# Two of the 64 score strips of a head get their exponentials on VectorE, with a new order of the strips, of the quantisation and of the FFN weight's decoding

## What is computed

```python
x = x + attn(layernorm(x))            # 8 key/value heads, each with 4 query groups, head size 16
x = x + ffn(layernorm(x))

# attn
q, k, v = x @ Wq.T, x @ Wk.T, x @ Wv.T
scores = einsum('bsqhd,bthd->bqhst', qh, kh) * 0.25
a_dot = softmax(scores) @ vh
a_mem = elu(q) @ memory / (elu(q) @ memory_norm)
out = a_dot * (1 - w) + a_mem * w     # w = sigmoid(memory_weight)

# ffn: one 512x512 product
x_fp8 = clip(x / s).astype(float8_e4m3fn)
y = (x_fp8 * s) @ (weight_fp8 * weight_scale).T
```

## Time and profile before

| what | value |
|---|---|
| three runs | 2145.21, 2145.61, 2146.34 us; median 2145.61 |
| the profiled execution's own time | 2146.34 us |
| its span, first to last instruction | 2144.2 us |
| mean granted TensorE clock | 0.994 |
| ScalarE busy | 1991.7 us (93%) |
| PE matmul records busy | 2086.2 us (97%) |
| VectorE busy | 483.7 us (23%) |
| GpSimd busy | 71.2 us (3%) |
| exponentials (L590) | 2112 instructions, 1882.6 us busy |
| scores (L692) | 16384 matmuls, 1149.5 us busy |
| weighing by v (L703) | 8192 matmuls, 1058.4 us busy |

### The profile page before, as it was taken

How to read it: one execution, slowest core, us unless ns; L and a number is a source line. 1 busy time by engine, 2 the same in 40 slices (tenths; PEclk the granted TensorE clock), 3 DMA queues, 4 the chain that set the end, 5 groups by cost and what they waited for, 6 DMA issues and landing times.

```text
span 2144.2 us, 65931 instructions
## 1 busy us (share of the span) xinstructions
PE 2086.2 (97%) x27314; PEld 779.5 (36%) x27314; DVE 483.7 (23%) x1006; ACT 1991.7 (93%) x2308; POOL 71.2 (3%) x93
## 2 busy tenths in 40 slices
PE   7999799999999999999999999999999999999996
PEld 4555333333333333333333333333333333333332
DVE  5666410013011311131110311130112211131104
ACT  4544699999999999999999999999999999999995
POOL 3222000000000000000000000000000000000000
PEclk9999899999999999999999999999999999999998
DMA  5554311111111211121111211111112111121111
GB/s 185 174 178 139 108 46 46 44 45 31 40 44 44 64 34 30 44 64 44 44 32 37 64 44 44 41 46 41 44 44 64 39 30 44 44 64 44 27 37 40
DMA packets 119531, 124.69 MB, mean 58 GB/s; under 512 B 13696, under 2 KB 96000, under 8 KB 119488
## 3 DMA queue, kind: packets, MB, share of 16 engines
q1 hardware_dynamic: 117424, 121.42, 20.6%
q10 hardware_dynamic: 2064, 2.69, 0.4%
HBM read 86.57 MB, written 37.49 MB: 58 GB/s over the span
## 4 chain that ended last, share of the span: by engine, by line
PE 68%; ACT 14%; issue 13%; DVE 3%; SPq 1%; DMA 0%; POOL 0%; DVEq 0%; ACTq 0%
PE ps L692 32%; PE ps L703 28%; ACT pool L590 13%; PE ps L640 4%; PE ps L735 1%; PE ps L654 1%; DVE pool L833 1%; PE ps L616 1%; DVE parts L858 0%; DVE norm L862 0%; DVE y_out L920 0%; SPq L299 0%; SPq L311 0%; DMA y_out<-in_Wq 0%; DVE ps L925 0%
## 5 line engine op out<-in xcount | busy, mean ns | idle before, releaser
L590 ACT ACTIVATE pool<-ps 128x1024 f32<-128x1024 f32 (+1 forms) x2112 | 1882.6, 1172 | 13.9 <-PE ps L692 13.6
L692 PE MATMUL ps<-q_st,k_st 99*32 99x512 bf16 x16384 | 1149.5, 380 | 13.7 <-DMA v_st<-v_aug 10.1
L703 PE MATMUL ps<-pool,v_st 128*32 128x512 f32 x8192 | 1058.4, 592 | 0.7 <-ACT pool L590 0.7
L692 PEld LDWEIGHTS ps<-q_st,k_st 99*32 99x32 bf16 x16384 | 375.1, 95 | 988.2 <-ACT pool L590 673.8
L703 PEld LDWEIGHTS ps<-pool,v_st 128*32 128x32 f32 x8192 | 247.2, 111 | 205.3 <-ACT pool L590 1.6
L1006 DVE STREAM_TRANSPOSE by_token<-ps 128x512 f32<-128x512 f32 x64 | 45.9, 717 | 421.6 <-PE ps L703 421.6
L1092 DVE RECIPROCAL rnorm<-ps 128x2 f32<-128x2 f32 x64 | 10.9, 170 | 519.1 <-PE ps L735 519.1
L1060 DVE SCALAR_TENSOR_TENSOR y_out<-ps,scalars,resid 128x512 f32 x28 | 21.0, 751 | 449.8 <-PE ps L721 449.8
L640 PE MATMUL ps<-pool,wqT 128*128 128x512 f32 x256 | 113.9, 592 | 0.0
L546 ACT ACTIVATE parts<-ps 128x512 bf16<-128x512 f32 x40 | 23.9, 597 | 75.6 <-PE ps L640 75.6
L640 PEld LDWEIGHTS ps<-pool,wqT 128*128 128x128 f32 x256 | 47.9, 190 | 52.5 <-issue 50.2
(11 more groups left out here) (114 smaller groups left out, 599.3 us busy)
## 6 DMA issues: line engine op xcount, KB each, us to landing
q_st<-q_aug SPq DMA_DIRECT2D x384, 64.0 KB
v_st<-v_aug SPq DMA_DIRECT2D x64, 256.0 KB
...
```

Of the source, the lines that this page charges most:

```text
L590: act.activation(probs[:, j % PTILES, q * CH:(q + len(strips)) * CH], sc[v % SLOTS][:, 0:len(strips), :].rearrange("p a b -> p (a b)"), AC ...
L692: last = pe.matmul(sc[u % SLOTS][VW * c:VW * c + VW, x, :], k_st[0:AUG, par, keys:keys + VW], q_st[0:AUG, par, q * CH:q * CH + CH], start= ...
L703: last = pe.matmul(acc[par][VW * c:VW * c + VW, :].rearrange("v (i s) -> v i s", s=VW), v_st[:, par, j, :], by_place[:, c, :, :], start=(j ...
```

## The change

Units. The table of a head's units is now a list of 33 triples (tile, first strip, number of strips). Tiles 0, 1 and 2 come first (units 0 to 5), then tile 15 ("late") as unit 6 with two strips and units 7 and 8 with one strip each, then tiles 3 to 14 (units 9 to 32). ScalarE takes the 31 units with two strips. Units 7 and 8 are VectorE's: `late_exps` reads each strip from PSUM (with a maximum against a lower limit), which frees its slot, and then computes the exponentials of both strips at once, 128x1024, with two instructions of one input and six of two inputs. `slot_free` says whom PE waits for before it overwrites a slot. ScalarE's scale is changed and W_k is scaled to fit, so that VectorE can build a power of two from the score directly.

Order. The weighing of tile 15 is moved to unit 26, between those of tiles 9 (at 25) and 10 (at 27); the other places are in `WEIGH_AT`. The ring has 3 tiles and one place of its own for tile 15. The memory products go to units 11 and 24, the FFN's transposition to unit 6 and its products to units 9, 11, 12 and 14.

Quantisation. VectorE rounds a tile of 128 tokens in each pair of heads, between the two halves of the memory term; GpSimd works out one tile's standard deviation at a time. The weight is decoded by a quarter (128x512) in each of the chunks 1 to 4 of the preparation, and is transposed by PE and copied by ScalarE after the last chunk. The polynomial's scratch lies over `parts`, so VectorE waits for the stores of `parts` before the heads.

The diff, cut to its core:

```diff
+LATE = 2
 SLOTS = 3
-UNIT_STRIPS = [(i, i + 1) for i in range(0, STRIPS - UNIT, UNIT)] + [(STRIPS - 2,), (STRIPS - 1,)]
+LATE_TILE = ST - 1
+BEFORE_LATE = 3
+RING = 3
+
+
+def units_of_head():
+    def halves(j):
+        return [(j, 0, 2), (j, 2, 2)]
+
+    units = [u for j in range(BEFORE_LATE) for u in halves(j)]
+    units += [(LATE_TILE, 0, 2), (LATE_TILE, 2, 1), (LATE_TILE, 3, 1)]
+    return units + [u for j in range(BEFORE_LATE, LATE_TILE) for u in halves(j)]
+
+
+UNIT_STRIPS = units_of_head()
 UNITS = len(UNIT_STRIPS)
-PTILES = 4
...
+BY_ACT = [u for u, (_, _, n) in enumerate(UNIT_STRIPS) if n == 2]
+BY_DVE = [u for u, (_, _, n) in enumerate(UNIT_STRIPS) if n == 1]
+HEAD_EXPS = len(BY_ACT)
+LAST_UNIT = {j: u for u, (j, _, _) in enumerate(UNIT_STRIPS)}
+
+WEIGH_AT = {4: 0, 6: 1, 10: 2, 26: LATE_TILE} | {LAST_UNIT[j] + SLOTS: j for j in range(BEFORE_LATE, LATE_TILE)}
...
+DECODE_STEPS = 8
+FLOAT8_STEPS = 6
+FFN_TURN_AT = 6
+FFN_PRODUCT_AT = (9, 11, 12, 14)
+MEMORY_AT = (11, 24)
...
-        probs = pool[:, 0:PTILES * QG * CH].rearrange("p (a b) -> p a b", a=PTILES)
+        probs = pool[:, 0:RING * QG * CH].rearrange("p (a b) -> p a b", a=RING)
+        late_probs = pool[:, RING * QG * CH:(RING + 1) * QG * CH]
...
+        late = parts[:, :, :, :].rearrange("p o i s -> p (o i s)").bitcast(F32)
+        late_x, late_z, late_p = (late[:, i * LATE * CH:(i + 1) * LATE * CH] for i in range(3))
...
-                act.activation(dst, src, ACT.Copy).then_inc(w_copied, 1)
+                act.activation(dst, src, ACT.Copy, scale=SCALE / EXP_UNIT if j == KT else 1.0).then_inc(w_copied, 1)
...
+                else:
+                    for k in range(KT):
+                        act.wait_ge(wf_turned, k + 1)
+                        act.activation(wT_ffn[:, k, :], weight_tp[k % 2], ACT.Copy).then_inc(wf_copied, 1)
...
-                    strips = UNIT_STRIPS[v % UNITS]
-                    j, q = divmod(strips[0], QG)
-
-
-                    act.wait_ge(scores_ready, pair * (2 * UNITS) + v + 1)
-                    act.activation(probs[:, j % PTILES, q * CH:(q + len(strips)) * CH],
-                                   sc[v % SLOTS][:, 0:len(strips), :].rearrange("p a b -> p (a b)"), ACT.Exp,
-                                   scale=SCALE).then_inc(probs_ready, 1)
+                for par in range(2):
+                    for a, u in enumerate(BY_ACT):
+                        j, q, n = UNIT_STRIPS[u]
+                        held = late_probs if j == LATE_TILE else probs[:, j % RING, :]
+
+
+                        act.wait_ge(scores_ready, pair * (2 * HEAD_EXPS) + par * HEAD_EXPS + a + 1)
+                        act.activation(held[:, q * CH:(q + n) * CH], sc[u % SLOTS].rearrange("p a b -> p (a b)"), ACT.Exp,
+                                       scale=EXP_UNIT).then_inc(probs_ready, 1)
...
+                    turn_ffn_weight()
+
+            def turn_ffn_weight():
+                pe.wait_ge(dec, KT * DECODE_STEPS)
+                for k in range(KT):
+                    if k >= 2:
+                        pe.wait_ge(wf_copied, k - 1)
+                    for a in range(KT):
+                        last = pe.transpose(weight_tp[k % 2][:, a * P:a * P + P], w_val[:, a, k * P:k * P + P], ident_bf[:, :])
+                    last.then_inc(wf_turned, 1)
...
+            def slot_free(n, u):
+                v = (u - SLOTS) % UNITS
+                heads_back = 1 if u < SLOTS else 0
+                if v in BY_DVE:
+                    pe.wait_ge(late_taken, n * LATE + BY_DVE.index(v) + 1)
+                else:
+                    pe.wait_ge(probs_ready, n * HEAD_EXPS + BY_ACT.index(v) + 1 - heads_back * HEAD_EXPS + THREE_FREE)
+
...
-                pe.wait_ge(probs_ready, n * UNITS + u - SLOTS + 1 + THREE_FREE)
-                for x, strip in enumerate(UNIT_STRIPS[u]):
...
+                last.then_inc(late_scores if u in BY_DVE else scores_ready, 1)
...
+                if j == LATE_TILE:
+                    pe.wait_ge(late_ready, n + 1)
+                held = late_probs if j == LATE_TILE else probs[:, j % RING, :]
...
+                        if u in WEIGH_AT:
+                            weigh_v(n, par, WEIGH_AT[u])
+                        elif u + UNITS in WEIGH_AT and not (first and par == 0):
+                            weigh_v(n - 1, 1 - par, WEIGH_AT[u + UNITS])
...
+            def decode_weight(a):
+                first = a * DECODE_STEPS
+                mag, sign, twice = (work[:, 4 + i, :] for i in range(3))
+                if a == 0:
+                    dve.wait_ge(w8_loaded, 16)
...
+                dve.tensor_tensor(w_val[:, a, :], mag, sign, ALU.mult).then_inc(dec, 1)
...
+                    if o == 3 and 1 <= c < 1 + KT:
+                        decode_weight(c - 1)
...
+            for o in range(QG + 1):
+                dve.wait_ge(parts_stored[o], 16 * SPLIT * (NG + 1))
+
+            def late_exps(n):
+                for d, u in enumerate(BY_DVE):
+                    dve.wait_ge(late_scores, n * LATE + d + 1)
+                    dve.tensor_scalar(late_x[:, d * CH:d * CH + CH], sc[u % SLOTS][:, 0, :], LOWEST, None, ALU.max)\
+                        .then_inc(late_taken, 1)
+                dve.wait_ge(late_taken, n * LATE + LATE)
+                dve.tensor_scalar(late_z, late_x, ROUND, None, ALU.add).then_inc(late_step, 1)
+
+                dve.wait_ge(late_step, n * LATE_STEPS + 1)
+                dve.scalar_tensor_tensor(late_x, late_z, ROUND, late_x, ALU.subtract, ALU.subtract).then_inc(late_step, 1)
+
+
+                dve.wait_ge(late_step, n * LATE_STEPS + 2)
+                dve.tensor_scalar(late_z.bitcast(I32), late_z.bitcast(I32), 23, LEADING_BITS,
+                                  ALU.logical_shift_left, ALU.bitwise_or).then_inc(late_step, 1)
+                dve.scalar_tensor_tensor(late_p, late_x, POWER[4], late_x, ALU.add, ALU.mult).then_inc(late_step, 1)
+                for i in (3, 2, 1):
+                    dve.wait_ge(late_step, n * LATE_STEPS + 7 - i)
+                    dve.scalar_tensor_tensor(late_p, late_p, POWER[i], late_x, ALU.add, ALU.mult).then_inc(late_step, 1)
+                dve.wait_ge(late_step, n * LATE_STEPS + LATE_STEPS)
+                dve.scalar_tensor_tensor(late_probs[:, LATE * CH:2 * LATE * CH], late_p, POWER[0], late_z, ALU.add, ALU.mult)\
+                    .then_inc(late_ready, 1)
...
+                dve.tensor_tensor(xq_now[:, :], xs, big, ALU.subtract).then_inc(xq_ready, 1)
...
+            with dve.Fori(0, HEADS // 2) as hp:
+                late_exps(2 * hp)
+                add_memory(0, hp, 0)
+                add_memory(0, hp, 1)
+                add_head(2 * hp, 0, 0, 2 * hp)
+                late_exps(2 * hp + 1)
+                add_head(2 * hp + 1, 1, 0, 2 * hp + 1)
...
             with dve.Fori(1, NG) as g:
-                round_to_float8(g - 1)
                 with dve.Fori(0, HEADS // 2) as hp:
-                    add_memory(g, hp)
-                    next_ffn_tile(g - 1, hp)
+                    late_exps(g * HEADS + 2 * hp)
+                    add_memory(g, hp, 0)
+                    round_to_float8(g - 1, hp)
+                    add_memory(g, hp, 1)
                     add_head(g * HEADS + 2 * hp, 0, g, 2 * hp)
+                    take_turned(g - 1, hp)
+                    late_exps(g * HEADS + 2 * hp + 1)
                     ffn_out(g - 1, hp)
                     add_head(g * HEADS + 2 * hp + 1, 1, g, 2 * hp + 1)
             chunk_moments(NG - 1)

```

More of the change, by code:

```diff
@@ L1 @@
+import math
 from contextlib import ExitStack
@@ L158, in attention_ffn @@
         tp = [ps[:, i, :] for i in (0, 1)]
+        weight_tp = [ps[:, i, 0:CH // 2].bitcast(BF16) for i in (0, 1)]
         pj = [ps[:, i, :] for i in (2, 3, 5, 6)]
@@ L162, in attention_ffn @@
         k_norm = (vp[:, 0:1], n2[:, 0:1])
-        sc = [ps[:, UNIT * i:UNIT * i + UNIT, :] for i in range(SLOTS)]
+        sc = [ps[:, 2 * i:2 * i + 2, :] for i in range(SLOTS)]
         acc = [ps[:, i, :] for i in (6, 7)]
@@ L684, in _ @@
                 pe.wait_ge(gm_loaded, 16 * QK_LOADS * (NG * HEADS + 1) + 32)
+            def slot_free(n, u):
[3 more added lines that the diff above has]
+                    pe.wait_ge(late_taken, n * LATE + BY_DVE.index(v) + 1)
+                else:
+                    pe.wait_ge(probs_ready, n * HEAD_EXPS + BY_ACT.index(v) + 1 - heads_back * HEAD_EXPS + THREE_FREE)
             def scores(n, par, u):
-                pe.wait_ge(probs_ready, n * UNITS + u - SLOTS + 1 + THREE_FREE)
-                for x, strip in enumerate(UNIT_STRIPS[u]):
-                    j, q = divmod(strip, QG)
+                slot_free(n, u)
+                j, q0, count = UNIT_STRIPS[u]
+                for x in range(count):
+                    q = q0 + x
                     for c in range(P // VW):
@@ L737, in memory_products, with pair @@
                 last.then_inc(am_ready, 1)
-            def turn_ffn_weight(k):
-                if k == 0:
```

(31 more changed lines are left out.)

164 lines of the change are left out of this document (72 added, 92 removed).

## The result

The changed kernel takes **2178.96 us** (median of 4 runs, 2176.77 to 2179.47), the kernel before 2145.58 in the runs beside it: a ratio of 1.0153, 95% interval 1.0136 to 1.0171. It is slower by 33 us, where 19 were forecast. The profiled execution took 2179.47 us with a span of 2177.8; before, these were 2146.34 and 2144.2. So some 33.5 us of the span are to be explained.

The account below looks back on a forecast made before the run. ScalarE was taken as the bound, PE close behind. Heads +11.1, preparation +8 and smaller terms +0.2 on the profiled 2146.34 us gave 2165.6, median put at 2165 us, range 2150 to 2182.

Parts of the forecast that it names:

- The restart behind unit 6: Each head: ScalarE has nothing after unit 6 until unit 9 is written; 0.82 us lost a head, 1.64 a pair.
- The slack: Scores' lead over ScalarE runs out: 0.45 us lost near units 27-28 of first heads, 0.10 and 0.13 in second heads.
- VectorE's slots and its arithmetic: In the heads: strip reads free slots tight but on time, cost 0; arithmetic hidden with 5 us to spare.
- The preparation: Chunks 1 to 4: 4.4 us of decoding makes PE 2.0 us late four times, +8 us (bounds +4 and +14).
- The smaller terms: Weight's transposition after the last chunk 0.4, transpositions gone from second head -0.7, first head's memory product +0.5; together +0.2 us.
- The strips simply leave ScalarE: Rival, heads: unit 9 ready when 6 ends, a head takes 28.43 us, whole 2091; 4%.
- Only the restarts count: Rival, heads: slack outside unit 9 holds, -10 us; with the preparation 2144, no change; 8%.
- Late slots: Rival, heads: VectorE's reads come 1 us later, units 10 and 11 wait in 28 pairs, +28 us, 2193; 8%.
- The clock falls in the new gaps: Rival, heads: PE idles behind unit 8; five or six per cent of the heads at half speed would make 2250; 4%.

Follow-up runs that it names:

- e2: Changed kernel with VectorE's second single strip one unit later (units 7 and 9 instead of 7 and 8): 2160.53 us, 1.0068 of the kernel before.
- e7: Changed kernel with decoding at the chunks' end, VectorE's single strips at units 10 and 14, weighings, memory halves and FFN pieces moved: 2123.16 us (0.9897).
- e3: Changed kernel's new order of units and weighings, but ScalarE computes the two single strips instead of VectorE: 2185.13 us, 1.0180 of the kernel before.
- e5: Changed kernel with tile 15 weighed behind unit 30 instead of unit 26: 2170.40 us, 1.0108 of the kernel before.
- e1: Changed kernel with VectorE's polynomial left out, strips still read and ones written instead: 2179.15 us, 1.0154 of the kernel before.
- e8: Changed kernel with the last four of each chunk's eight decoding instructions moved to the chunk's end: 2167.24 us, 1.0093 of the kernel before.
- e6: Changed kernel with PE's loop over pairs 1 to 3 written out straight: 2173.79 us, 1.0129 of the kernel before.
- e10: Changed kernel without the back-edge hint on PE's loop over pairs 1 to 3: 2173.04 us, 1.0121 of the kernel before.

## Why the prediction was right, and where its sum was off

The sign, the range (2150 to 2182) and the mechanism in the heads held; the point, 2165, was 14 us low. Of these, 6.2 lie in the preparation, 5.9 at head 8, which the sum didn't have, and 2 in the pairs. That the range held in spite of head 8 is partly luck: its upper end was meant for slow reads by VectorE and slow decoding.

- **The restart behind unit 6: right.** 0.05 + 0.66 + 1.02 gave 0.82 a head; it is 0.83, and the gap has PE's scores as releaser. e2 moved it as the reckoning says and e7 took most of it away.
- **The slack: right in its places, close in its sizes.** Units 27 and 28 of a first head: 0.07 and 0.38 forecast, 0.09 and 0.38 measured. Second head with FFN, units 11 and 28: 0.10 and 0.13 forecast, 0.11 and 0.18 measured. With them a pair is 59.23 us, 59.16 forecast. e3 and e5 tested the stalls alone.
- **VectorE's slots and its arithmetic: right.** A read took 0.68, a two-input instruction 1.22 or 1.23. e1 shows that nothing waits for the arithmetic.
- **The preparation, +8 for +14.6: the mis-sized term.** "4.4 us with the waits" was 4.96, inside its bounds of 3.4 to 5.9, because GpSimd's square ran beside one of the eight instructions (+0.73). A chunk also had only 2.3 us to spare for it (e8 loses 0.45 with 2.71 of decoding), not 2.4. So it lost 2.7 us instead of 2.0 (4 x 2.7 = 10.8). The clock is the step that was missing, and it took the whole past the upper bound of +14: 2 x 1.7 = 3.4 more in two chunks, after waits of 2.54 and 2.75 us. I had weighed the clock's fall in the heads alone. 0.3 was lost before the first decoding.
- **The smaller terms.** The row for the weight's transposition says 0.40 us, not 0.33, which moves the sum by about 0.1. Heads 0 and 1 took 0.3 us more, where 0.1 was forecast.
- **Head 8, +5.9: not in the sum.** The loop's exit and its hint are not in the diff, and the trace of before shows no stand there. e6 and e10 show that it hangs on the exit of the loop; why it came with this change stays open.
- **Rivals.** "The strips simply leave ScalarE" falls with the gap before unit 9. "Only the restarts count" falls with e3 and e5. Late slots don't occur: in the heads PE's matmuls wait for ScalarE, for loads or on "issue", never for VectorE. "The clock falls in the new gaps": in the heads behind head 8 it is 1.00 with PE idle 0.52 us at a time, so the case that the Trainium skill ("TensorE: Matmul & The Clock Gate", A second HAM failure mode) describes doesn't show here. Where it fell, PE had stood at least 2.08 us at a stretch (e8, head 0), and behind other such stands it didn't fall.
